# One predicated copy of 1024 elements in place of two of 512 in the second sort of a graph network kernel

## The reference

```python
edge_index = jnp.stack([src, dst])
x = _layernorm(x + _L0_gnn_ref(x, edge_index, ...))               # softmax by source, sum by target
x = _layernorm(x + _L1_gnn_ref(x, edge_index, edge_weight, ...))  # weighted sum by target
x = _layernorm(x + _L2_gnn_ref(x, ..., src, dst, edge_type_32, ...))  # attention by (type, target)
x = _layernorm(x + _L3_gnn_ref(x, edge_index, ...))               # softmax and sum by target
```

## Time and profile before

| what | value |
|---|---|
| median of 3 runs | 6948.78 us (6944.86 to 6948.97) |
| profiled execution | 6950.12 us, span of the trace 6948.3 us |
| busy share of the span: PE, DVE, ACT, POOL | 15%, 56%, 14%, 70% |
| second sort's network on DVE | about 358 to 987 us |
| block of the second sort, POOL's fetches and look-ups | about 353 to 1192 us |

### The profile page before, as it was taken

How to read it: one execution, slowest core, us unless ns; L and a number is a source line. 1 busy time by engine, 2 the same in 40 slices (tenths; PEclk the granted TensorE clock), 3 DMA queues, 4 the chain that set the end, 5 groups by cost and what they waited for, 6 DMA issues and landing times. The chain is left out here.

```text
span 6948.3 us, 28978 instructions
## 1 busy us (share of the span) xinstructions
PE 1022.4 (15%) x4502; PEld 687.2 (10%) x4502; DVE 3900.6 (56%) x7989; ACT 994.5 (14%) x2479; POOL 4855.7 (70%) x4956
## 2 busy tenths in 40 slices
PE   6403247000000000000067840000000001000000
PEld 5403235000000000000033310000000001000000
DVE  8999998444544443443346677777433444333336
ACT  1022233000000100000044520000000013222223
POOL 0078777677777677777767777777777777777774
PEclk9996569555555555555579975555555555555555
DMA  3090001244444343443348973333434432333332
GB/s 57 3 379 7 2 11 19 47 106 112 110 107 112 98 114 103 107 105 103 97 140 324 334 245 117 116 94 97 104 104 107 105 87 64 109 109 103 109 109 70
DMA packets 556803, 772.07 MB, mean 111 GB/s; under 512 B 122155, under 2 KB 433249, under 8 KB 537033
## 3 DMA queue, kind: packets, MB, share of 16 engines
q0 software_dynamic: 159120, 283.64, 18.3%
q1 hardware_dynamic: 379284, 375.57, 16.7%
q10 hardware_dynamic: 18210, 111.02, 4.0%
HBM read 357.68 MB, written 412.16 MB: 111 GB/s over the span
## 5 line engine op out<-in xcount | busy, mean ns | idle before, releaser
L2486 POOL DMA_INDIRECT l2s_krow<-table_k,l2s_idx x784 | 775.3, 989 | 261.9 <-issue 258.5
L940 POOL DMA_INDIRECT l2z_rows<-proj,l2z_idx x784 | 764.5, 975 | 250.5 <-issue 238.3
L940 POOL DMA_INDIRECT l0z_rows<-table,l0z_idx x784 | 743.6, 948 | 249.1 <-issue 238.6
L788 POOL DMA_INDIRECT l3z_rows<-table,l3z_idx x784 | 739.8, 944 | 249.4 <-issue 225.5
L940 POOL DMA_INDIRECT l1z_rows<-table,l1z_idx x784 | 739.7, 943 | 247.7 <-issue 238.6
L1929 POOL DMA_INDIRECT first_sj<-scores,first_atdst x544 | 592.5, 1089 | 181.9 <-issue 181.9
L2441 PE MATMUL l2s_bank<-l2o_wr,l2s_fed 128*128 128x512 f32 x800 | 383.5, 636 | 114.4 <-ACT l2s_fed L2465 98.8
L973 DVE TENSOR_TENSOR l1z_msg<-l1z_rows,l1z_factors 128x1024 f32<-128x1024 f32 (+1 forms) x50 | 60.0, 1200 | 553.3 <-DMA l1z_rows<-table,l1z_idx 553.2
L2423 DVE SCALAR_TENSOR_TENSOR l2s_qrow<-l2s_qrow,g_dokeep,l2s_zrow 128x82 f32<-128x82 f32 x1568 | 345.3, 296 | 6.4 <-DMA l2s_qrow<-table_q,l2s_first 5.7
L973 DVE TENSOR_TENSOR l2z_msg<-l2z_rows,l2z_factors 128x1024 f32<-128x1024 f32 (+1 forms) x50 | 60.0, 1200 | 511.5 <-DMA l2z_rows<-proj,l2z_idx 511.0
L759 DVE SCALAR_TENSOR_TENSOR l3z_acc<-l3z_acc,l3z_xx,l3z_msg 128x128 f32<-128x128 f32 x784 | 272.8, 348 | 83.7 <-ACT l3z_msg L778 57.7
(11 more groups left out here) (583 smaller groups left out, 5076.6 us busy)
## 6 DMA issues: line engine op xcount, KB each, us to landing
proj<-l2s_proj ACTq DMA_DIRECT2D x100, 1024.0 KB, 4.9
spread_q<-prep_zero SPq DMA_DIRECT2D x98, 656.0 KB
l2s_zrow<-spread_q SPq DMA_DIRECT2D x98, 656.0 KB, 4.0
prefix<-l0z_acc SPq DMA_DIRECT2D x196, 256.0 KB, 3.2
prefix<-l1z_acc SPq DMA_DIRECT2D x196, 256.0 KB, 3.0
prefix<-l2z_acc SPq DMA_DIRECT2D x196, 256.0 KB
prefix<-l3z_acc SPq DMA_DIRECT2D x48, 1040.0 KB, 4.1
l0z_rows<-table,l0z_idx POOLq DMA_INDIRECT x784, 2.6
```

Of the source, the lines that this page charges most:

```text
L788: nc.gpsimd.indirect_dma_start(out=rows[:, k % RING, u, :], out_offset=None, in_=table, in_offset=bass.IndirectOffsetOnAxis(ap=idx[:, lo + ...
L940: nc.gpsimd.indirect_dma_start(out=rows[:, k % RING, c * (hi - lo) + u, :], out_offset=None, in_=table, in_offset=bass.IndirectOffsetOnAxi ...
L2486: nc.gpsimd.indirect_dma_start(out=krow[:, h, u, :], out_offset=None, in_=g.table_k, in_offset=bass.IndirectOffsetOnAxis(ap=idx[:, h, u:u ...
```

## The change

In straight stages, and in flips of block 2 (where a flip is the same as a straight stage), one predicated copy of 1024 elements does the work of the two. Its destination is the whole new payload row, seen as (block, half, element). Its source is the old payload with the two halves of every block swapped, by a step of -1 over the halves. The mask of 512 elements is read for both halves, by a step of 0. It adds 2 to `paid`. The 15 other flips keep their two copies.

```diff
                 eng.wait_ge(self.masked, n)
                 eng.wait_ge(self.copied, n)
-                v.copy_predicated(new_w_lo, swap, w_hi).then_inc(self.paid, 1)
-                v.copy_predicated(new_w_hi, swap, w_lo).then_inc(self.paid, 1)
+                if kind == "straight" or arg == 2:
+                    pairs = [w.rearrange("p (n t h) -> p n t h", t=2, h=arg // 2) for w in (self.pay[1 - at % 2], self.pay[at % 2])]
+                    both = swap.unsqueeze(2).to_broadcast([P, WIDE // arg, 2, arg // 2])
+                    v.copy_predicated(pairs[0], both, pairs[1][:, :, ::-1, :]).then_inc(self.paid, 2)
+                else:
+                    v.copy_predicated(new_w_lo, swap, w_hi).then_inc(self.paid, 1)
+                    v.copy_predicated(new_w_hi, swap, w_lo).then_inc(self.paid, 1)
```

## The result

The changed kernel takes 6975.08 us, the median of 5 runs (6968.52 to 6977.26), against 6948.78 us: a ratio of 1.0037, 95% interval 1.0024 to 1.0049. That is slower by 26 us. The profiled execution took 6977.26 us, with a span of 6975.5 us.

A forecast was written before the change was run, and what follows sets the result against it. POOL's fetches and spreads bound the block: 926 us (sort) + 229 (177 fetches) + 64.5 (spreads, gap) = 1219.5 against 1192.0; 6950.1 + 27.5 = 6977.6, profiled 1.3 above median, so 6976 us. Range 6950 to 7010.

The forecast's parts named there:

- POOL ends the block, DVE's gain does not come through: Block's end: DVE's sort ends 62 us earlier, but DVE waits for POOL and the block ends 27.5 us later.
- Two fetches per changed stage, one of them held until the copy is over: Second sort from 548 us: two POOL fetches per 2.98 us stage, 1.49 us each, where it was five in two stages.
- Rivals 3 and 4: 3: new copy doesn't hold POOL, 6934 us, chance 0.09; 4: half held, five fetches per two stages, 6940 to 6960, 0.14.
- The copy's price: DVE's sort: the 1024-element copy has a pitch of 1.14 us at all block sizes; sort ends near 925.
- Blocks 2 and 4 get fast because the destination has no holes: 44 stages of the sort: predicated writes with holes were slow; 44 x (2.27 - 1.14) = 50 us go.
- rivals 1 and 2: 1: blocks 2 and 4 stay slow, 7004 us, chance 0.12; 2: new pattern slow everywhere, about 7088 us, 0.04.
- That pause ends when the zeros do: POOL up to 548 us: one 27.88 us fetch ends with SP's zeros, so a slower POOL loses nothing there.
- The sum: Block's end: 926 + 229 + 64.5 = 1219.5 us against 1192.0, 27.5 us later.
- Rival 5: DVE alone set the block's end, so all 62 us come through: 6887 us, chance 0.03.

The follow-up runs named there:

- e4: The changed kernel with 32 columns moved from POOL's fetches to the look-ups: 6933.8 us, ratio 0.9973.
- e11: The changed kernel plus a one-element DVE memset in every stage of the second sort: 6963.8 us, ratio 1.0013.
- e8: The kernel before plus a one-element DVE memset in every stage of the second sort: 6946.6 us, ratio 0.9985.
- e3: The changed kernel with the mask in PSUM instead of SBUF: 7034.5 us, ratio 1.013.
- e7: The changed kernel with POOL's fetches begun only after the sort's last predicated copy: 7446.9 us in one run.
- e6: The kernel before; in straight stages of block 2 and 4, first copy has holes only in its source, second only in its destination: 6950.7 us, one run.
- e1: The changed kernel with the single copy only in blocks 2 and 4, two copies elsewhere: 6933.9 us, ratio 0.997.
- e5: The kernel before; in straight stages of block 2 and 4, two copies split by row half, each with a one-run destination: 6932.7 us, ratio 0.9963.
- e9: The kernel before with copies halved by row in blocks 2 and 4, plus a one-element memset in every stage: 6904.5 us, ratio 0.9922.
- e12: The changed kernel with single copies in blocks 2 and 4 alone, plus a one-element memset in every stage: 6917.5 us, ratio 0.9944.
- e2: The changed kernel with the single copy only in blocks of 8 and more: 6973.4 us, ratio 1.0031.
- e10: The kernel before with copies halved by row in blocks 2 and 4, plus a one-element memset in every fourth stage: 6903.5 us, ratio 0.9922.

## Why the prediction was right, and where it was lucky

The forecast was 6976 us, and 6975.08 us were measured.

- *POOL ends the block, DVE's gain does not come through.* Shown by e4, which gives DVE work for its idle time and so brings the next block 43 us forward.
- *Two fetches per changed stage, one of them held until the copy is over.* Right: 891.28 and 1.47 us, as said. Measured alone (e11 against e8) the single copy adds 601.3 - 558.6 = 42.7 us to the fetches. Rivals 3 and 4, no hold or half of it, fall. The Trainium skill (SBUF — State Buffer, "Who interferes with whom") has a DVE instruction with two SBUF inputs contend with a GpSimd instruction that reads SBUF: e3's fetches in mid-copy (0.94 against 1.47 us) agree. The Trainium skill infers there that descriptor generation needs the write side alone, so that a `tensor_tensor` does not stall it: here e3's mask, a `tensor_tensor`, held fetches for 1.43 and 2.68 us. What such a fetch reads in SBUF no run shows.
- *The copy's price.* I took 1.14 us; it is 1.18 to 1.21 alone (e7) and 1.18 to 1.25 beside the fetches. The sort ended at 940, not 926. Since POOL ends the block, this cost little: the sort had more stretch for fetches (380 done, not 367), and 14 us at 1.54 us a fetch in place of 1.295 are an estimated 2 us.
- *Blocks 2 and 4 get fast because the destination has no holes.* Right, by e6; rivals 1 and 2 fall.
- *"That pause ends when the zeros do, not when DVE does. [...] So a slower POOL loses nothing here."* This step failed. The 27.88 us of the earlier trace rows were a fetch passed over by DVE, as e8 shows with the zeros in place; and fetches of 9.0 to 17.6 us came at 688, 701 and 895 (e1, changed, e5), long after the zeros. Nothing fixes that pause: the changed kernel had its own long fetches, 8.2 and 10.7 us, and lost 617.9 - 601.3 = 16.6 us to them, the kernel before 33.9.
- *The sum.* 42.7 of hold less 17.3 of luck with long fetches make the 25.4 us that were measured, near my 27.5. Two wrong steps met in it: I charged no hold before 548 us, where POOL did lose some (133 fetches begun by then in e11, 143 in e8), and foresaw no relief there, where it got more than that back (127 instructions up to 548, not 118). Within the sort I had 1.52 us a fetch; it was 1.54 with the long one, 1.51 without (e11).
- *Rival 5, DVE's queue alone,* falls: DVE stands idle for 80.5 us at the block's end. The Trainium skill advises (VectorE: DVE Perf Modes, "Rules for kernel authors") to minimize the count of DVE operations: here fewer operations meant fewer boundaries for POOL. e9 and e12 differ in nothing but that count in 44 stages, and in e9, with two copies for one, the next block starts 11.4 us earlier (the medians lie 13 us apart).

Outside e3, all fetches over 2.1 us are among the first four behind one of POOL's pauses (last section), which shift it against DVE, and they come out at another length in each kernel. They may be part of what spreads the runs of one kernel (e5's lie 16 us apart, e9's with memsets 5), but not all of it: e11's, with memsets too, lie 15 us apart.

Open is why a waiting fetch is passed over at forty and more boundaries between DVE instructions, at each of which other fetches are served, and which breaks other than the memset let it in. Five such fetches end 0.82 to 0.83 us after DVE fell idle: for 0.03 us ahead of L147 (e5, e1 and the changed kernel's first), for 0.9 us in the changed kernel (712.1), for 0.6 us in e5 (912.9). Two were let in behind the first slow copy that they met (before, 543.8, and e6, 536.8), and one behind a single copy of 1024, after it had been passed over behind four others (e2, 533.3).

## What to carry to other kernels

Before two instructions are made one, ask who lives in the gap between them: here, where POOL issued indirect DMAs beside a DVE that never paused, what POOL got was set by DVE's instruction boundaries. In such a kernel the row of that engine's busy time by line prices the change better than DVE's own. A memset of one element in each stage of this sort, full of instructions with two SBUF inputs, cost at most 1.3 us in all and took away waits of up to 29 us. For predicated copies the form whose destination is one run, at the length of its neighbours, was the best one here (e9).

## What the runs showed of the hardware beyond that

- A predicated copy of 512 floats has a pitch of 0.60 to 0.68 us with a source with holes and a destination of one run (e5, e6), 1.07 to 1.12 us the other way round (e6); one of 1024 into one run 1.18 to 1.21 us alone (e7), at every block size, with a step of -1 in the source and a step of 0 in the mask.
- POOL pauses when 113, 226, 385 and 498 of its fetches are done, at the same four places in every kernel: 7.1 to 7.3 us the first time, and 3.0 to 3.9 us the others. Where the first came after SP's zeros (e3, e7), it too was 3.1 to 3.3 us.
- The next block begins 8.8 us after POOL's last spread where POOL is last (the changed kernel, e1 to e3, e5 to e7, e11, e12), but 6.2 us in e4, for a reason that stays open. Where DVE is last (e8 to e10), it begins 1.15 us after DVE's last instruction.
